# Linear attention: one table places the steps of a sequence, and ScalarE normalizes x

## The reference

```python
def _layernorm(x, axis=-1, eps=1e-05):
    m = jnp.mean(x, axis=axis, keepdims=True)
    v = jnp.var(x, axis=axis, keepdims=True)
    return (x - m) / jnp.sqrt(v + eps)
...
    def _L1_attn_ref(x, qkv_w, qkv_b, out_w, out_b):
        ...
        q_prime = jax.nn.elu(q) + 1.0
        k_prime = jax.nn.elu(k) + 1.0
        kv_prod = jnp.einsum('bhld,bhle->bhlde', k_prime, v)
        kv_cumsum = jnp.cumsum(kv_prod, axis=2)
        context = jnp.einsum('bhld,bhlde->bhle', q_prime, kv_cumsum)
        k_cumsum = jnp.cumsum(k_prime, axis=2)
        norm = jnp.einsum('bhld,bhld->bhl', q_prime, k_cumsum)
        output = context / (norm[..., None] + EPS)
        output = output.transpose(0, 2, 1, 3).reshape(b, l, e)
        return output @ out_w + out_b
...
    h = _layernorm(x, axis=-1) * (1 + ca) + sa
    x = x + ga * _L1_attn_ref(h, ...)
```

## Time and profile before

| | us |
|---|---|
| time, median of 3 runs (1328.81 to 1330.93) | 1330.33 |
| the profiled execution's own time | 1328.92 |
| its span | 1327.0 |
| PE busy, share of the span | 1121.3 (84%) |
| DVE busy | 744.3 (56%) |
| ACT busy | 566.0 (43%) |
| POOL busy | 457.4 (34%) |
| linear attention: first to last of its instructions, about | 766 to 1066 |

### The profile page before, as it was taken

One profiled execution on the slowest core, in us unless ns is written; L12 is line 12 of the kernel. 1 busy time (PEld: TensorE's weight loads), 2 busy tenths in 40 slices (PEclk: granted clock), 3 DMA queues, 4 the chain that ended last, 5 costly groups with the idle time before them and its releaser, 6 DMA issues. The chain is left out here.

```text
span 1327.0 us, 19347 instructions
## 1 busy us (share of the span) xinstructions
PE 1121.3 (84%) x6462; PEld 593.2 (45%) x6462; DVE 744.3 (56%) x1538; ACT 566.0 (43%) x1025; POOL 457.4 (34%) x668
## 2 busy tenths in 40 slices
PE   6279999999999991598989638999999929999996
PEld 5134445554544430354545315666666613333332
DVE  3167778788787745223223237777777623464543
ACT  0227676676776661123223213333333204545543
POOL 0345446445454310478877523222223100000000
PEclk7669999999999995699999859999999969999997
DMA  4134134233252213266666430111110020012000
GB/s 169 30 58 77 26 70 93 46 75 85 39 90 58 43 50 105 72 128 155 130 151 132 75 99 1 37 37 37 37 41 17 21 91 1 8 56 64 0 32 32
DMA packets 73042, 85.26 MB, mean 64 GB/s; under 512 B 12520, under 2 KB 67560, under 8 KB 72688
## 3 DMA queue, kind: packets, MB, share of 16 engines
q1 hardware_dynamic: 60656, 67.23, 19.8%
q0 software_dynamic: 12288, 16.79, 7.7%
HBM read 45.54 MB, written 25.47 MB: 54 GB/s over the span
## 5 line engine op out<-in xcount | busy, mean ns | idle before, releaser
L655 DVE TENSOR_REDUCE nmax<-psum 128x1 f32<-128x512 f32 (+3 forms) x352 | 215.5, 636 | 51.9 <-PE psum L847 46.5
L759 ACT ACTIVATE pT<-psum 128x512 f32<-128x512 f32 x320 | 181.1, 596 | 66.7 <-PE psum L866 36.6
L845 PE MATMUL psum<-k6T,q6T 96*128 96x512 bf16 (+3 forms) x512 | 128.2, 310 | 14.3 <-DVE nmax L655 10.2
L863 PE MATMUL psum<-q6T,k6T 99*128 99x512 bf16 x320 | 119.4, 382 | 1.1 <-ACT pT L759 0.9
L1084 POOL DMA_INDIRECT residual<-expert_y,idx_e x64 | 101.2, 1581 | 37.6 <-DVE expert_y L1206 21.1
L2029 PE MATMUL psum<-c_state,c_w 128*128 128x512 f32 x192 | 102.5, 636 | 0.1
L847 PE MATMUL psum<-negs_bf,ident_bf 128*128 128x128 bf16 (+2 forms) x352 | 88.8, 252 | 0.0
L845 PEld LDWEIGHTS psum<-k6T,q6T 96*128 96x128 bf16 x512 | 45.7, 99 | 88.0 <-DVE nmax L655 55.5
L878 PE MATMUL psum<-pT,v 128*32 128x512 f32 x640 | 85.1, 604 | 0.0
L1487 DVE TENSOR_TENSOR l_scores<-psum,const_sb 128x512 f32<-128x512 f32 x128 | 79.1, 679 | 10.0 <-PE psum L1639 10.0
L1071 POOL DMA_INDIRECT expert_tokens<-router_input,idx_e x64 | 63.7, 995 | 54.3 <-POOLq L947 35.2
(11 more groups left out here) (234 smaller groups left out, 2259.1 us busy)
## 6 DMA issues: line engine op xcount, KB each, us to landing
q6T<-q_parts SPq DMA_DIRECT2D x96, 128.0 KB, 4.5
expert_w<-in_ew SPq DMA_DIRECT2D x16, 768.0 KB
x_in<-in_x SPq DMA_DIRECT2D x8, 512.0 KB, 4.0
residual<-x SPq DMA_DIRECT2D x32, 128.0 KB, 1.8
router_input<-h SPq DMA_DIRECT2D x32, 128.0 KB, 1.8
l_x<-residual SPq DMA_DIRECT2D x8, 512.0 KB, 4.2
x_dram<-l_x SPq DMA_DIRECT2D x32, 128.0 KB, 3.5
c_x<-x_dram SPq DMA_DIRECT2D x4, 1024.0 KB, 6.0
```

The lines of the kernel that those rows point to most:

```text
L655: dve.tensor_reduce(nmax[:, i, u * nh:(u + 1) * nh], ps_s[:, n % SR, 0:nh * (i + 1) * P].rearrange("p (h k) -> p h k", h=nh), AX_X, ALU.ma ...
L759: act.activation(pT[:, n % PR].rearrange("p h t -> p (h t)"), ps_t[:, n % TR, :], ACT.Exp, scale=HD ** -0.5).then_inc(probs, 1)
L845: pe.matmul(out[:, a, :], q6T[0:6 * HD, b % 2, u * nh + a, i * P:(i + 1) * P], k6T[0:6 * HD, b % 2, 0:w], start=a == 0, stop=False, skip_g ...
L863: last = pe.matmul(out, k6T[:, b % 2, j * P:(j + 1) * P], q6T[:, b % 2, hg * 4:hg * 4 + 4, i * P:(i + 1) * P], start=True, stop=j < i)
```

## The change

`linear_main` and `linear_order` go. In their place stand a table, `LINEAR_PLACE`, that gives each step of a sequence a place, and a sort: step s of sequence b comes at `36 * b + place(s)`. `placed_order` is what `attention_order` was, made general; the attention's table keeps its numbers under a new name, so its order stays as it was. And the step xn moves from DVE to ACT: an activation computes `rstd * x + nbias`, and POOL makes `nbias = -mean * rstd` with two more operations in st.

```diff
+LINEAR_STEPS = 36
+LINEAR_PLACE = {
+    "ln": -322,
+    "st": -318,
...
+    "nt": -262,
+    "nb": [-255, -249],
+    "A": [-258, -252, -242, -233],
...
-    order = linear_order()
+    order = placed_order(LINEAR_PLACE, LINEAR_STEPS, linear_steps(), B)
...
-                        pool.tensor_tensor(rstd[:], vtmp[:], mhalf[:], ALU.pow).then_inc(rstd_ready, 1)
+                        link(pool.tensor_tensor(rstd[:], vtmp[:], mhalf[:], ALU.pow))
+                        link(pool.tensor_tensor(vtmp[:], mv[:, :, 0], rstd[:], ALU.mult))
+                        pool.tensor_scalar(nbias[:], vtmp[:], -1.0, None, ALU.mult).then_inc(nbias_ready, 1)
...
-                    if s[0] == "xn":
-                        b = s[1]
-                        dve.wait_ge(rstd_ready, b + 1)
-                        if b:
-
-                            dve.wait_ge(x_fill, x_use[("hT", b - 1, 1)] + 1)
-                        for i in range(NT):
-                            dve.tensor_scalar(xn[:, i, :], x_in[:, b % 3, i, :], mv[:, i, 0:1], rstd[:, i:i + 1],
-                                              ALU.subtract, ALU.mult).then_inc(xn_ready, 1)
...
+                    if s[0] == "xn":
+                        b = s[1]
+                        act.wait_ge(nbias_ready, b + 1)
+                        if b:
+
+                            act.wait_ge(x_fill, x_use[("hT", b - 1, 1)] + 1)
+                        for i in range(NT):
+                            act.activation(xn[:, i, :], x_in[:, b % 3, i, :], ACT.Identity, bias=nbias[:, i:i + 1],
+                                           scale=rstd[:, i:i + 1]).then_inc(xn_ready, 1)
```

More of the change, by code:

```diff
@@ L156, in mix @@
     return out + b[n:]
-PLACE_STEPS = 136
-PLACE = {
+ATTENTION_STEPS = 136
+ATTENTION_PLACE = {
     "ln": -197,
@@ L181, with placed_order, place @@
 }
+def placed_order(table, count, steps, sequences):
+    def place(s):
+        at = table[s[0]]
+        for n in s[1:]:
+            at = at[n]
+        return at
+    assert len(steps) == count
+    order = [(count * b + place(s), (s[0], b) + s[1:]) for b in range(sequences) for s in steps]
+    return [s for _, s in sorted(order)]
 def attention_steps():
@@ L193, in attention_steps @@
     return steps
[L196 to L207, removed]
 def index_of(order, kinds):
@@ L340, in attention_phase @@
 def attention_phase(nc, m):
-    order = attention_order()
+    order = placed_order(ATTENTION_PLACE, ATTENTION_STEPS, attention_steps(), B)
     x_use, _ = index_of(order, ("hT", "kT", "mT", "oC", "h2T", "lg"))
@@ L1206, in _, with linear_steps @@
                         dve.tensor_tensor(y[:, e % YS, i, :], yw[:, i, :], m.gb_rows[:, i, :], ALU.mult).then_inc(gated, 1)
[L1208 to L1233, removed]
+LINEAR_STEPS = 36
+LINEAR_PLACE = {
+    "ln": -322,
+    "st": -318,
+    "xn": -303,
+    "hT": [-296, -289],
+    "qk": [-279, -273, -281, -277],
+    "v": [-283, -280, -275, -270],
+    "mask": [-276, -264],
+    "nt": -262,
+    "nb": [-255, -249],
+    "A": [-258, -252, -242, -233],
+    "kt": [-271, -265, -232],
+    "KV": [-251, -238, -225],
+    "PV": [-248, -236, -227, -221],
+    "pr": [-230, -223, -220, -218],
+}
+def linear_steps():
+    steps = [("ln",), ("st",), ("xn",), ("nt",)]
+    steps += [(kind, n) for kind in ("hT", "mask", "nb") for n in range(2)]
+    steps += [(kind, n) for kind in ("qk", "v", "A", "PV", "pr") for n in range(4)]
+    return steps + [(kind, n) for kind in ("kt", "KV") for n in range(NT - 1)]
 def head_pairs(v):
@@ L1273, in linear_phase @@
         vtmp = sb("l_vtmp", [P, NT])
+        nbias = sb("l_nbias", [P, NT])
         xn = sb("l_xn", [P, NT, C])
@@ L1310, in linear_phase @@
         pool_steps = sem("lin_pool_steps")
-        rstd_ready = sem("lin_rstd_ready")
+        nbias_ready = sem("lin_nbias_ready")
         xn_ready = sem("lin_xn_ready")
```

## The result

| | before | after |
|---|---|---|
| median | 1330.37 us (1328.81 to 1330.93) | 1299.18 us (1298.03 to 1300.17) |
| ratio, 95% interval | | 0.9767 [0.975, 0.9784] |
| the profiled execution, its span | 1328.92, 1327.0 us | 1298.03, 1296.2 us |
| a sequence in the middle, hT 0 to hT 0 | 34.09 us | 30.45 us |

The change gains 31.2 us. The direction is right, the size is too small.

A forecast was written before the change was run, and what follows sets the result against it. Waits of PE's in-order queue on top of its own work were taken as the bound. New parts 0.8 + 50.5 + 155.5 + 30.0 + 24.7 = 261.5 us against 286.3 gain 24.8: median 1305.5 us, range 1300 to 1317.

The forecast's parts named there:

- The three waits of the earlier trace: PE's losses per sequence before: 2.29 us from A1 to nb0, 0.45 from kt2 to v1, 0.55 from A0 to nt.
- PE's own work, 30.8 us, and 0.3 us of waits behind it: A middle sequence: 34.09 us less 3.29 of waits, the floor of any order, plus 0.3 of new waits: 31.1 us.
- five full sequences: The middle of linear attention: 5 x 34.09 = 170.5 us before, 5 x 31.1 = 155.5 us new.
- rival 5: More gain: PE at its floor of 30.8 us a sequence and the tail shorter too, 1301 us; chance 0.05.
- the tail: From the last nt to the phase's end: 24.6 us before, 24.7 new, no gain.
- Sequences 0 and 1: The phase's first two sequences: 58.2 us before, 50.5 new (21.6 and 28.9).
- the last hT0 to nt: Last sequence, from its hT0 to its nt: 33.0 us before, 30.0 new.
- The start: Phase start: POOL's two added operations for nbias have nothing to hide behind, +0.8 us once.
- The load of x: Load shortly ahead of st: lands as st is due, cost taken as 0; DVE waits at most 0.5 us.
- rival 3: Slower: st waits for its load, 1335 us at a 12 us landing; sign: DVE wait over 1 us; chance 0.03.
- xn on ACT: Four activations, 2.07 us a sequence, 0.59 each, beside other work: ACT at 14.2 us, DVE down to about 22.6.
- Rival 1: The table trades waits for waits; only DVE's relief of 2.33 us ahead of nb0 counts: 1316 us; chance 0.17.

The follow-up runs named there:

- after_again: The kernel after, unchanged, run a second time: 1300.17 us, ratio 0.9753.
- experiment 5: The run ln_late, a later issue of the loads of x against the kernel after: 1313.2 us.
- experiment 1: Each half alone: xn on ACT in before's order, one slot earlier, 1336.3 us; after's order with xn on DVE, 1307.97 us.
- ln_late: The kernel after, with the loads of sequences 3 to 7 also waiting until v0 of the sequence before is drained: 1313.2 us, ratio 0.9853.
- nt_late: The kernel after, with nt moved in the table from -262 to -256, behind A0: 1332.49 us, ratio 1.0004.
- wait_lump: The kernel after, plus nine DVE memsets of an unused tile ahead of the copy of nt's sums, each sequence: 1358.58 us, ratio 1.0192.
- wait_split: The kernel after, plus twelve DVE memsets of an unused tile in four groups of three, each sequence: 1343.33 us, ratio 1.0075.
- only_order: The kernel after in its new order, but with xn computed by DVE and without nbias: 1307.97 us, ratio 0.9812.

## Why the prediction was right, and where it fell short

- *What bounds the kernel.* Right. The three waits of the earlier trace rows were the loss, and the order with xn moved removes all of them.
- *PE's own work, 30.8 us, and 0.3 us of waits behind it.* This is the step that failed. A sequence takes 30.45 us, 0.65 less than the 31.1, and five full sequences 3.3 us less. Of the 0.65 us, 0.3 were waits of a tenth at pr3 and nt that I put in and that did not come. The other 0.35 us is the floor itself. The 30.8 was got by taking three visible losses off 34.09, so it carries the distances from step to step of the old order, and those are not the same in the new one. At two places the old order seems to hold a small wait with no idle time printed, first in before (the qk ahead of this v starts at 917.99), then the same steps in after:

```profile
919.87 1.13 PE L1603 MATMUL psum<-l_w,l_hT 128*128 128x256 f32 x4
...
936.39 1.08 PE L1673 MATMUL psum<-l_scores,l_v 128*32 128x128 f32 x32
937.53 1.13 PE L1603 MATMUL psum<-l_w,l_hT 128*128 128x256 f32 x4
```

```profile
870.34 1.08 PE L1674 MATMUL psum<-l_scores,l_v 128*32 128x128 f32 x32
871.35 1.13 PE L1604 MATMUL psum<-l_w,l_hT 128*128 128x256 f32 x4
872.32 1.88 PE L1598 MATMUL psum<-l_hT,l_w 128*128 128x512 f32 x4
874.04 1.03 PE L1604 MATMUL psum<-l_w,l_hT 128*128 128x256 f32 x4
874.98 1.98 PE L1598 MATMUL psum<-l_hT,l_w 128*128 128x512 f32 x4
876.89 1.15 PE L1640 MATMUL psum<-l_q_masked,l_k 32*128 32x256 f32 x16
```

  qk to v takes 1.88 us there and 1.72 here, PV to v 1.14 and 1.01. But the new order has long distances of its own, 1.82 us from another qk to its v (877.97), 1.91 from qk to A2 (874.98) and 1.13 from PV2 to nt, so these two places don't make the difference. It is spread over several forms, and some went the other way. The sums of one sequence, start to start, for before (from 906.93) with its three losses taken off, and for after (from 860.38):

  | step | before, us | after, us |
  |---|---|---|
  | qk, four | 7.24 | 7.17 |
  | A, four | 4.32 | 4.31 |
  | PV from the scores, four | 4.17 | 4.16 |
  | v, four | 3.88 | 3.73 |
  | pr, four | 3.66 | 3.66 |
  | nb, two | 1.99 | 1.81 |
  | PV from the state, three | 1.63 | 1.71 |
  | KV, three | 1.42 | 1.55 |
  | hT, two | 1.06 | 1.00 |
  | kt, three | 0.85 | 0.77 |
  | nt | 0.58 | 0.57 |
  | together | 30.80 | 30.44 |

  Which of these differences were waits, and which come only from the step that follows, no run shows. Pricing each form by its shortest distance in before does not give the floor either: it gives 29.8 us, 0.6 too low, where the prices of the prediction gave 30.8, 0.4 too high.
- *The range.* Its low end was rival 5, PE at its floor, worked out at 1301 from the 30.8. With the measured 30.45 that rival is what happened, and the end should have been some 2 us lower, and lower again for the scatter in the last point. The profiled execution came out 6.1 us under its own forecast (1298.03 against 1304.1): 3.3 in the five full sequences, 0.9 in the first two, 0.7 in the last, 0.7 the other way at the start and in the tail, and 2.0 outside the phase. Without those 2.0, which are scatter, the time would have been at about 1301, inside the range, as after_again was with 1300.17. So the step above explains why the size was off; that the time lies just outside the range is in part luck.
- *Sequences 0 and 1.* 49.65 us measured, 50.5 forecast; *the last hT0 to nt*, 29.33 and 30.0; *the tail*, 24.93 and 24.7. Right within 0.9 us.
- *The start.* 1.3 us later than before (15.8 against 14.5 from the phase's first load to the first transpose), not 0.8. One part is POOL: its power operation stands beside DVE's map now (below).
- *The load of x.* Right that it costs PE nothing, with too small a margin in the numbers: DVE waits about 1 us in two of five sequences, where at most 0.5 was forecast. One of them, 1.06 us, even passes the prediction's own sign for rival 3, and cost nothing: the cover is 2.2 us and not 1.9 (experiment 5).
- *xn on ACT.* 0.59 us each as forecast, ACT 13.8 us a sequence against 14.2, and no wait of A0 for its mask. DVE is busy for 23.3 to 23.5 us and not 22.6; why stays open.
- *Rival 1, only xn counts.* It falls, and so does its opposite: the 2x2 of experiment 1 shows that order and xn are worth 2.36 and 0.25 us alone, 3.64 together.
- *Rival 3, slower.* The mechanism is real, 2.2 us a sequence in ln_late, but the load of the change is not near that point. A likelier way to the other side had no place among the rivals: a wait at nt to nb0 that also costs the clock. In nt_late 2.4 us of waits a sequence and four sequences with a fallen clock gave the whole gain back.
- *The phases around it.* 2.0 of the 31.2 us lie outside linear attention: it starts at 764.47 us instead of 766.01, with the same program ahead, and the rest behind it takes 0.45 us less. That is scatter and not the change: the phase started at 766.50 in after_again, and anywhere from 762.9 to 769.8 in the other kernels above, all with the same program ahead.

The 30.8 us by which the span of the profiled execution fell add up so: -1.3 at the start, 8.6 in sequences 0 and 1, 18.2 in the five full ones, 3.6 in the last up to nt, -0.3 in the tail, and 2.0 around it.

## What to carry to other kernels

A floor made by taking the visible waits off a measured period is a floor of that order: short waits that show no idle time stay in it, and so do distances that change with the step that follows. Give it a lower bound too, from the shortest start-to-start distance of each form; here the two were 30.8 and 29.8 us, with 30.44 measured between them. Two edits that clear one chain can be worth little alone and much together, because each only hands the wait to the other; judge them as a pair. And in a table of places, keep what feeds TensorE early enough that its waits stay short as well as few, and don't lie close together: one wait of 4.1 us cost 6.9 us a sequence here, and four of 0.6 to 1.5 us cost 5.0.

## What the runs showed of the chip

- In wait_lump TensorE's granted clock fell from 2.4 to 1.2 GHz during a wait of 4.1 us, in each full sequence, and in the one shown some 5.5 us of work behind it ran at half speed; 1.8 to 2.9 us were lost on top of the wait. Waits of 0.6 to 1.5 us, four in a sequence, left the clock at 1.00 in wait_split's full sequences. Two waits of 1.06 and 1.26 us whose ends are 2.4 us apart brought it down in some sequences of nt_late and not in others.
- A power operation of POOL on 128x4 values took 1.04 us before and 1.56 to 1.82 us after. What runs beside it is another thing in the two (its durations in ns, min/median/max, first in before and then in after; then the timeline of after):

```profile
L1376 POOL TENSOR_TENSOR l_rstd<-l_vtmp,l_mhalf x5: 1036/1036/1037, 861.8 to 998.2; 128x4 f32<-128x4 f32 x5
```

```profile
L1375 POOL TENSOR_TENSOR l_rstd<-l_vtmp,l_mhalf x5: 1562/1570/1822, 845.3 to 967.1; 128x4 f32<-128x4 f32 x5
```

```profile
875.87 0.66 DVE L1447 SCALAR_TENSOR_TENSOR l_k<-l_exp,l_plus_one 128x512 f32<-128x512 f32 x1
...
876.57 1.22 DVE L1454 TENSOR_TENSOR_SCAN l_k_sums<-l_ones,l_k 128x512 f32<-128x512 f32 x1
876.80 1.82 POOL L1375 TENSOR_TENSOR l_rstd<-l_vtmp,l_mhalf 128x4 f32<-128x4 f32 x1 [0.18 <-POOL l_vtmp L1374]
```

  In after it meets DVE's operations with two inputs in SBUF; in before it ran beside the masks (L1487), which read one of their inputs from PSUM. The Trainium skill, page "SBUF — State Buffer", section "Who interferes with whom", says that an operation of VectorE with two inputs in SBUF and a GpSimd operation that reads SBUF exclude each other. The rows agree with that as far as one pair can; no run here isolates it.
- xn on DVE reads one tensor, so that sentence does not cover it, and yet it too is long beside POOL. In before one of xn's four pieces takes 1.36 us where POOL's multiply by the running sum (L1402, 1.41 us from 937.51) starts beside it, and the others 0.40. In only_order all pieces from 834 us on take 0.40, away from that multiply; the one group that meets it (804.63, POOL at 804.53) has a piece of 1.32.
